# Attention in a small vision tower: ScalarE reads a pair of projection pieces in one instruction where their two PSUM banks are neighbours

## The chip, the core and the metric

The kernel runs on one core of a Trainium2 chip. The core has five engines that run side by side and meet at semaphores: TensorE (PE, matmuls, with its weight loads, PEld), VectorE (DVE), ScalarE (ACT), GpSimd (POOL) and SyncE (SP, which here only issues DMAs). TensorE writes its sums to PSUM, 8 banks of 512 fp32 numbers per partition. The metric is the time of one execution on the device in microseconds, as the median of several runs.

## The reference, cut to what matters

A batch of 64 images goes through a patch embedding, one attention layer with fake quantisation and one feed-forward layer. D = 192, 12 heads of 64, N = 197 tokens per image.

```
h = tok(x, W, b); h = concat([cls_tok, h], axis=1)              # (64, 197, 192)
a = layernorm(h)
qkv = fake_quant(a, sx1, zx1) @ fake_quant(ww1, sw1, zw1).T     # 3 x 768 columns
q, k, v = split(qkv), heads of 64
p = softmax(fake_quant(q) @ fake_quant(k).T * scale)
o = fake_quant(p, sa, za) @ fake_quant(v, sv, zv)
h = h + (fake_quant(o, sx2, zx2) @ fake_quant(ww2, sw2, zw2).T + bb2)
h = h + ffn(layernorm(h))
```

fake_quant(t, s, z) rounds t / s, adds z, clips to 0..15, and goes back. The change lies in the line qkv: in how its sums leave PSUM.

## The kernel before

Three stages follow each other: the embedding (to about 235 us), attention (to about 860 us) and the feed-forward layer over pairs of 128-row tiles. The change is in attention.

Attention is a software pipeline over images. In image step b each engine goes through six slots u = 0..5, its instructions in a fixed order written out by hand, and works on several images at once: scores and exponentials of image b, v projection of image b + 1, q and k projections of images b + 2 and b + 3 (each even step makes q of two images, each odd step k), weighted values of b - 3, output projection of b - 5. Each engine has one queue in order.

*PSUM.* Banks 0 to 3 hold scores, bank 4 the softmax sums, and banks 5, 6, 7 all the rest, in turn. This rest are 14 pieces per step, in the order of the table SLOTS:

```
SLOTS = [[("y", 0, -5), ("qk", 0, 2), ("qk", 1, 2)],
         [("qk", 2, 2), ("qk", 3, 2), ("o", 0, -3)],
         [("qk", 4, 2), ("qk", 5, 2)],
         [("v", 0, 1), ("v", 1, 1), ("o", 1, -3)],
         [("v", 2, 1), ("v", 3, 1)],
         [("o", 2, -3)]]
def bank_of(b, n): return 5 + (NP * (b + 2) + n) % 3        # NP = 14
```

An entry is kind, number of the piece, and image relative to b. A qk piece is 128 x 394 (128 output channels, two images of 197 tokens), a v piece 128 or 69 tokens x 384 channels. So each step has five pairs of projection pieces, one in each of the slots 0 to 4.

*TensorE*, slot by slot (image_slot): in slot 0 first the output projection (L1213); then the pair of the slot (function projections: two matmuls over the first 128 of 192 input channels, L1197, then two over the last 64, L1200, which run side by side in two halves of the array); then the scores of the next unit (L1247); then in even slots the softmax sums (L1260), in odd ones the weighted values (L1230). In slot 5 the weighted values come first. Before each first matmul of a piece TensorE waits until ScalarE has read the piece that last stood in the bank (before, and the semaphores in the table evac, "qk_read" and "v_read"). The last matmul of a pair adds 2 to the semaphore in the table full.

*ScalarE*, slot by slot (image_step in its block): the exponential of unit u (L625, 788 columns out of two neighbouring banks), then the pieces of the slot one by one (read_piece: qk at L587, v at L596, y at L601, o at L606), each read scaled and rounded to int16 and each adding 1 to its evac semaphore.

*VectorE* clips the int16 numbers to 4 bits and makes them bf16 (L860): the qk pieces once all six are read, the v pieces once all four are. It also scales the probabilities (L1075), with a factor that comes through DRAM (z_row).

Of the kernel before, what the change touches and what calls it, by code (L numbers as in the profile page):

```python
# [5 lines left out]
def vit_tower_kernel(nc, xt, w_tok, tok_b, cls_tok, w1t, w2t, bb2, quant, w_in_t, g_in, w_out_t, g_out,  # L6
# [11 lines left out]
    ACT = mybir.ActivationFunctionType  # L18
    AX = mybir.AxisListType

    B, N, D = out.shape
# [14 lines left out]
    with ctx:  # L36
        def sb(name, shape, dt):
            return ctx.enter_context(nc.sbuf_tensor(name, shape, dt))

        def sem(name):  # L40
            return ctx.enter_context(nc.semaphore(name))

        def wait(eng, s, value):

            if isinstance(value, int) and value <= 0:
                return
            eng.wait_ge(s, value)
# [9 lines left out]
        psum = ctx.enter_context(nc.psum_tensor("psum", [128, 8, 512], fp32))  # L57
# [12 lines left out]
        F_Q, F_K, F_V, F_EXP, F_O, F_Y = range(6)  # L70
# [42 lines left out]
        qki = sb("qki", [128, 6, 2, N], i16)  # L113
        qkb = sb("qkb", [128, 2, 12, 2, N + 1], bf16)
        vi = sb("vi", [128, 2, 2, INNER], i16)
# [47 lines left out]
        evac = {k: sem(f"{k}_read") for k in ("qk", "v", "o", "y")}  # L163
# [134 lines left out]
        def exists(b, d):  # L298

            return 0 <= b + d < B  # L300

        def bank_of(b, n):

            return 5 + (NP * (b + 2) + n) % 3
# [234 lines left out]
        def _(act):  # L539
# [33 lines left out]
            def added(image, par):  # L573

                return 32 * ((image - par) // 2) if isinstance(image, int) else 16 * (image - par)

            def read_piece(b, par, n):
                kind, k, d = PIECES[n]
                if not exists(b, d):
                    return  # L580
                im, bank = b + d, bank_of(b, n)
                ip = im % 2
                act.wait_ge(full[kind], PER[kind] * im + k + 1)
                if kind == "qk":
                    if k == 0:
                        wait(act, s_qkb, b + 2)
                    act.activation(qki[:, k, :, :], psum[:, bank, 0:2 * N]  # L587
                                   .rearrange("p (c n) -> p c n", c=2), ACT.Copy,
                                   scale=factor[(F_Q, F_K)[b % 2]])\
                       .then_inc(evac[kind], 1)  # L590
                elif kind == "v":
                    t, half = k // 2, k % 2
                    r, W = TOK[t][1], INNER // 2
                    if k == 0:
                        wait(act, s_vb, im - 1)
                    act.activation(vi[0:r, ip, t, half * W:(half + 1) * W], psum[0:r, bank, 0:W], ACT.Copy,  # L596
                                   scale=factor[F_V]).then_inc(evac[kind], 1)
                elif kind == "y":
                    if im > 1:
                        wait(act, s_added[ip], added(im, ip))  # L600
                    act.activation(att[:, ip, :, :], psum[:, bank, 0:2 * D].rearrange("p (t d) -> p t d", t=2),  # L601
                                   ACT.Copy, scale=factor[F_Y]).then_inc(evac[kind], 1)
                else:
                    if k == 0:
                        wait(act, s_ob, im - 1)
                    act.activation(oi[:, ip, 2 * k:2 * k + 2, :], psum[:, bank, 0:2 * N]  # L606
                                   .rearrange("p (c n) -> p c n", c=2), ACT.Copy,
                                   scale=factor[F_O]).then_inc(evac[kind], 1)

            act.wait_ge(s_step, CONST_STEPS)  # L610
            factor = {}
# [4 lines left out]
            def image_step(b, par, tri):  # L616
                n = 0
                for u in range(U1):
                    U = U1 * b + u
                    if exists(b, 0):  # L620
                        g, t, r = u // 2, u % 2, TOK[u % 2][1]
                        act.wait_ge(s_scores, U + 1)
                        wait(act, s_pi, 2 * b - 5 + t)

                        act.activation(ex[0:r, tri, t, 4 * g:4 * g + 4, :].rearrange("p (a h) n -> p a h n", a=2),  # L625
                                       psum[0:r, 2 * t:2 * t + 2, 0:2 * N]
                                       .rearrange("p a (h n) -> p a h n", h=2), ACT.Exp,
                                       scale=factor[F_EXP]).then_inc(s_exp, 1)
                    for _ in SLOTS[u]:
                        read_piece(b, par, n)  # L630
                        n += 1
                    if b < 0:
                        if u == 0:
                            act.wait_ge(s_xb, JOIN + b + 1)
                            act.wait_ge(s_hp, JOIN + b + 1)
                        store_tile(JOIN + b, u)
# [787 lines left out]
```

## Time and profile before

| | us |
|---|---|
| median of 3 runs | 1194.58 |
| lowest and highest | 1193.99, 1195.8 |
| the profiled execution | 1195.78 |
| its span, first to last instruction | 1194.0 |
| TensorE, VectorE, ScalarE busy in the span | 1108.2, 1056.6, 923.6 |

The profile is of one execution. Times within it count from the start of the span. The page gives busy time for the whole; the stretches give it by stage; the timeline lists instructions in order of time, neighbours of one line merged, so that the second column is the time from the first start to the last end and x the number of instructions; the waits say which engine sat idle and who released it. An engine's rows can overlap: the end of one instruction lies over the start of the next.

### The profile page before, as it was taken

The page shows a single profiled execution, that of the slowest core. Times are in us where ns is not written, and L with a number is a line of the kernel's source. Part 1 is how long each engine was busy: PE and PEld are TensorE (multiplying, and loading weights), DVE is VectorE, ACT ScalarE, POOL GpSimd, SP SyncE. Part 2 cuts the span into 40 slices and gives each one's busy share as a digit, 9 for nine tenths or more (in the row PEclk, how much of TensorE's full clock was granted, in tenths as well). Part 3 has the DMA queues.
Part 4 walks back from the last instruction along what each step waited for, and adds up shares of the span by engine and source line. Part 5 has one row for each costly group of instructions (what it writes and reads, how often), then busy time and mean ns, then how long its engine had stood idle before and what let it go on. Part 6 is the DMA issues. An engine that isn't in the chain of part 4 may idle for free.

```text
span 1194.0 us, 32030 instructions
## 1 busy us (share of the span) xinstructions
PE 1108.2 (93%) x11210; PEld 674.9 (57%) x11210; DVE 1056.6 (88%) x2028; ACT 923.6 (77%) x1832; POOL 466.1 (39%) x498
## 2 busy tenths in 40 slices
PE   7999999889999999999999999999867888888887
PEld 6999998445555555555555555555534444444444
DVE  7687666599999999999999999999887999999996
ACT  0000001889999999999999999999637999999997
POOL 5644344302211223221111232221236777766774
PEclk9999999999999999999999999999879999999999
DMA  8998998445655566556555655555532333333332
GB/s 292 313 314 249 316 306 236 137 138 150 152 150 150 131 147 156 145 150 150 145 150 147 141 150 151 149 151 143 146 98 64 105 101 101 103 99 99 99 95 71
DMA packets 157284, 187.87 MB, mean 157 GB/s; under 512 B 42864, under 2 KB 118464, under 8 KB 156928
## 3 DMA queue, kind: packets, MB, share of 16 engines
q1 hardware_dynamic: 115680, 156.92, 42.2%
q0 software_dynamic: 15936, 10.88, 9.4%
q10 hardware_dynamic: 25536, 18.31, 4.8%
q8 instruction: 83, 1.36, 0.5%
q14 instruction: 49, 0.40, 0.2%
HBM read 143.11 MB, written 36.12 MB: 150 GB/s over the span
## 4 chain that ended last, share of the span: by engine, by line
PE 73%; ACT 10%; issue 7%; DMA 3%; DVE 3%; POOL 2%; SPq 1%; ACTq 1%; DVEq 0%; POOLq 0%
PE psum L1139 14%; PE psum L1197 12%; PE psum L1260 12%; PE psum L1230 7%; PE psum L1200 7%; PE psum L1213 6%; PE psum L1247 6%; PE psum L1326 5%; ACT yi L674 3%; ACT zi L682 2%; ACT big L667 2%; PE psum L1306 1%; PE psum L1316 1%; DMA big<-xt 1%; POOL big L797 1%
## 5 line engine op out<-in xcount | busy, mean ns | idle before, releaser
L1075 DVE TENSOR_TENSOR pi<-big 128x2364 int16<-128x2364 f32 (+1 forms) x128 | 333.8, 2608 | 13.5 <-DMA big<-z_row 13.0
L769 POOL DMA_DIRECT2D h_res<-att x128 | 146.8, 1301 | 492.7 <-ACT att L601 484.0
L625 ACT ACTIVATE big<-psum 128x788 f32<-128x788 f32 (+1 forms) x384 | 330.3, 862 | 5.1 <-PE psum L1247 2.8
L587 ACT ACTIVATE qki<-psum 128x394 int16<-128x394 f32 x384 | 172.4, 508 | 25.5 <-PE psum L1200 13.8
L1139 PE MATMUL psum<-big 128*128 128x192 f32 (+1 forms) x1128 | 185.0, 327 | 2.3 <-DMA big<-xt 2.0
L1139 PEld LDWEIGHTS psum<-big 128*128 128x128 f32 (+1 forms) x1128 | 180.3, 188 | 5.5 <-DMA big<-xt 2.6
L1260 PE MATMUL psum<-big,sa_hot 128*32 128x197 f32 (+1 forms) x3072 | 168.2, 336 | 0.6 <-DVE zt L1099 0.6
L587 ACT ACT_TABLE_LOAD x1 | 1.3, 1283 | 189.5 <-PE psum L1200 189.5
L797 POOL TENSOR_TENSOR big<-big,goutb 128x512 f32<-128x512 f32 (+1 forms) x99 | 123.8, 1270 | 59.5 <-DVE big L1042 59.4
L1247 PE MATMUL psum<-qkb 64*128 64x197 bf16 (+1 forms) x1536 | 128.9, 246 | 1.3 <-DVE qkb L860 1.3
L596 ACT ACTIVATE vi<-psum 128x384 int16<-128x384 f32 (+1 forms) x256 | 115.7, 529 | 4.0 <-PE psum L1200 3.7
L1230 PE MATMUL psum<-big,vb 128*64 128x197 bf16 (+1 forms) x1536 | 104.8, 259 | 14.8 <-issue 12.9
L860 DVE TENSOR_SCALAR big<-pi,lo,hi 128x2364 bf16<-128x2364 int16 (+1 forms) x128 | 114.9, 898 | 2.4
L606 ACT ACTIVATE oi<-psum 128x394 int16<-128x394 f32 x192 | 102.7, 536 | 18.2 <-PE psum L1230 18.1
L1197 PE MATMUL psum<-xT,w1b 128*128 128x394 bf16 x384 | 105.3, 334 | 4.9 <-ACT qki L587 2.1
L1260 PEld LDWEIGHTS psum<-big,sa_hot 128*32 128x32 f32 (+1 forms) x3072 | 80.8, 109 | 42.8 <-issue 0.8
L1288 PE MATMUL psum<-winb 96*128 96x512 bf16 x428 | 103.8, 386 | 0.0
L1326 PE MATMUL psum<-winb,big 96*128 96x512 bf16 (+1 forms) x396 | 96.9, 388 | 0.0
L1247 PEld LDWEIGHTS psum<-qkb 64*128 64x128 bf16 (+1 forms) x1536 | 76.4, 104 | 31.6 <-issue 11.4
L1230 PEld LDWEIGHTS psum<-big,vb 128*64 128x64 bf16 (+1 forms) x1536 | 62.2, 111 | 56.2 <-issue 53.4
L869 DVE TENSOR_TENSOR big<-psum,tokb 128x192 f32<-128x192 f32 x98 | 34.4, 351 | 56.5 <-PE psum L1139 56.1
L1197 PE MATMUL psum<-w1b,xT 128*128 128x384 bf16 (+1 forms) x256 | 72.7, 335 | 8.5 <-ACT vi L596 1.5
(109 smaller groups left out, 1812.6 us busy)
## 6 DMA issues: line engine op xcount, KB each, us to landing
big<-z_row SPq DMA_DIRECT2D x192, 394.0 KB, 5.0
big<-xt SPq DMA_DIRECT2D x98, 384.0 KB, 4.7
tin<-h_res SPq DMA_DIRECT2D x49, 192.0 KB, 3.0
tres<-h_res SPq DMA_DIRECT2D x49, 192.0 KB, 2.5
out<-oo SPq DMA_DIRECT2D x49, 192.0 KB, 2.6
h_res<-big ACTq DMA_DIRECT2D x84, 96.0 KB, 4.5
h_res<-att POOLq DMA_DIRECT2D x64, 96.0 KB, 3.4
x_int<-big ACTq DMA_DIRECT2D x84, 64.0 KB, 4.4
```

The source lines that it names most:

```text
L587: act.activation(qki[:, k, :, :], psum[:, bank, 0:2 * N] .rearrange("p (c n) -> p c n", c=2), ACT.Copy, scale=factor[(F_Q, F_K)[b % 2]])\
L596: act.activation(vi[0:r, ip, t, half * W:(half + 1) * W], psum[0:r, bank, 0:W], ACT.Copy, scale=factor[F_V]).then_inc(evac[kind], 1)
L625: act.activation(ex[0:r, tri, t, 4 * g:4 * g + 4, :].rearrange("p (a h) n -> p a h n", a=2), psum[0:r, 2 * t:2 * t + 2, 0:2 * N] .rearrang ...
L769: pool.dma_start(h_res[bass.ds(b - 4, 1), t0:t0 + r, :].rearrange("a n d -> (a n) d"), att[0:r, par, t, :], accum_op=ALU.add).then_inc(s_a ...
L797: g.tensor_tensor(yg[0:r, oth, a, :], yy[0:r, a, 0:HID], goutb[0:r, :], ALU.mult)\
L1075: v.tensor_tensor(pi[0:r, t, :, 0:N], ex[0:r, it, t, :, :], zb[0:r, ip, :, :], ALU.mult).then_inc(s_pi, 1)
L1139: last = mm(psum[p0:p0 + r, bank_of_tile(i, s), 0:D], xring[:, s, c * 128 + p0:c * 128 + p0 + r], weight_of(cls, c), start=(c == 0), stop= ...
L1197: mm(psum[rows, bank, 0:n], left[:, 0], right[:, 0], start=True, stop=False)
L1230: last = mm(psum[i * DH:(i + 1) * DH, bank, c * N:(c + 1) * N], vb[0:r, (tri + d) % 3, t, head * DH:(head + 1) * DH], pT[0:r, im % 2, t, j ...
L1247: last = mm(psum[0:r, 2 * (w % 2) + i % 2, (i // 2) * N:(i // 2 + 1) * N], qk[po:po + DH, 6 + c, t0:t0 + r], qk[po:po + DH, c, 0:N], start ...
L1260: last = mm(psum[32 * j:32 * j + 32, 4, 0:N], sa_hot[0:r, w // 2, :], ex[0:r, it, t, 4 * (w // 2) + j, :], start=(w == 0), stop=(w == 5))
L1326: last = mm(psum[0:r, 2 * a + half, :], zT3[:, oth, a, c, 0:r], winb[:, c, half * HID:(half + 1) * HID], start=(c == 0), stop=(c == 1))
```

## The change

read_piece, on ScalarE, now looks at the banks of a pair of qk or v pieces. Where the second bank is the one above the first (5,6 or 6,7), the first call reads both pieces in one instruction (PSUM operand and int16 operand both twice as long) and adds 2 to the evac semaphore at its end, and the second call returns after its wait. Where the banks are 7 and 5, the two reads stay apart. The o and y pieces are read as before. Nothing else of the kernel is edited: TensorE's order, its waits and what they wait for are the same.

```
             act.wait_ge(full[kind], PER[kind] * im + k + 1)
+            pieces = slice(k, k + 1)
+            if kind in ("qk", "v"):
+                together = bank_of(b, n - k % 2) < bank_of(b, n - k % 2 + 1)
+                if together and k % 2:
+                    return
+                pieces = slice(k, k + 1 + together)
+            count = pieces.stop - k
             if kind == "qk":
                 if k == 0:
                     wait(act, s_qkb, b + 2)
-                act.activation(qki[:, k, :, :], psum[:, bank, 0:2 * N]
-                               .rearrange("p (c n) -> p c n", c=2), ACT.Copy,
+                act.activation(qki[:, pieces, :, :].rearrange("p k c n -> p k (c n)"),
+                               psum[:, bank:bank + count, 0:2 * N], ACT.Copy,
                                scale=factor[(F_Q, F_K)[b % 2]])\
-                   .then_inc(evac[kind], 1)
+                   .then_inc(evac[kind], count)
             elif kind == "v":
-                t, half = k // 2, k % 2
+                t = k // 2
...
-                act.activation(vi[0:r, ip, t, half * W:(half + 1) * W], psum[0:r, bank, 0:W], ACT.Copy,
-                               scale=factor[F_V]).then_inc(evac[kind], 1)
+                act.activation(vi[0:r, ip, t, k % 2 * W:(k % 2 + count) * W].rearrange("p (k w) -> p k w", k=count),
+                               psum[0:r, bank:bank + count, 0:W], ACT.Copy,
+                               scale=factor[F_V]).then_inc(evac[kind], count)
```

ScalarE before, in the middle of any image step, from the reads of slot 1 (qk 2,3) to the exponential behind the v reads of slot 4 (qki: int16 of q and k; oi: of the weighted values; vi: of v; big: the exponentials):

```order
L587 ACTIVATE qki<-psum 128x394 x2
L606 ACTIVATE oi<-psum 128x394
L625 ACTIVATE big<-psum 128x788
L587 ACTIVATE qki<-psum 128x394 x2
L625 ACTIVATE big<-psum 69x788
L596 ACTIVATE vi<-psum 128x384 x2
L606 ACTIVATE oi<-psum 128x394
L625 ACTIVATE big<-psum 128x788
L596 ACTIVATE vi<-psum 69x384 x2
```

ScalarE after, the same place in a step where the first pieces of these pairs stand in banks 6, 6, 5, 5 (P2, P3, P4, P5 in the prediction's words, layout A):

```order
L594 ACTIVATE qki<-psum 128x788
L614 ACTIVATE oi<-psum 128x394
L633 ACTIVATE big<-psum 128x788
L594 ACTIVATE qki<-psum 128x788
L633 ACTIVATE big<-psum 69x788
L603 ACTIVATE vi<-psum 128x768
L614 ACTIVATE oi<-psum 128x394
L633 ACTIVATE big<-psum 128x788
L603 ACTIVATE vi<-psum 69x768
```

All four pairs of these slots have become one instruction each. The next step, from the same place (banks 5, 5, 7, 7; layout B):

```order
L594 ACTIVATE qki<-psum 128x788
L614 ACTIVATE oi<-psum 128x394
L633 ACTIVATE big<-psum 128x788
L594 ACTIVATE qki<-psum 128x788
L633 ACTIVATE big<-psum 69x788
L603 ACTIVATE vi<-psum 128x384 x2
L614 ACTIVATE oi<-psum 128x394
L633 ACTIVATE big<-psum 128x788
L603 ACTIVATE vi<-psum 69x384 x2
```

In this step the qk reads are joined and the v reads, whose banks are 7 and 5, are not. The step after it (banks 7, 7, 6, 6; layout C):

```order
L594 ACTIVATE qki<-psum 128x394 x2
L614 ACTIVATE oi<-psum 128x394
L633 ACTIVATE big<-psum 128x788
L594 ACTIVATE qki<-psum 128x394 x2
L633 ACTIVATE big<-psum 69x788
L603 ACTIVATE vi<-psum 128x768
L614 ACTIVATE oi<-psum 128x394
L633 ACTIVATE big<-psum 128x788
L603 ACTIVATE vi<-psum 69x768
```

Here it is the other way round: the qk reads of slots 1 and 2 stand apart, the v reads are joined. The reads of qk 0,1 in slot 0 are joined in the second and third of these steps. The three kinds of step repeat to the end of attention. In all, 129 pairs of qk and 86 pairs of v are read by one instruction, of 192 and 128.

## Rows read from the trace of the kernel before

**Rows 1.** The page: busy us (share of the span) and instructions of each engine
```profile
PE 1108.2 (93%) x11210; PEld 674.9 (57%) x11210; DVE 1056.6 (88%) x2028; ACT 923.6 (77%) x1832; POOL 466.1 (39%) x498
```

**Rows 2.** Stretches: us, busy us (instructions) by engine, granted clock, DMA share, GB/s
```profile
400.00:500.00 100.00, 98.02 (x1276) 51.96 (x1274) 96.90 (x100) 97.61 (x198) 28.56 (x20) 1.00 0.62 149
```

**Rows 3.** Line 596 in 260 to 838 us: durations in ns, first and last start
```profile
L596 ACT ACTIVATE vi<-psum x232: 503/527/552, 260.9 to 837.6; 128x384 int16<-128x384 f32 x58, 69x384 int16<-69x384 f32 x58
```

**Rows 4.** Timeline of ScalarE, one image: start us, us to the last end, line, shapes
```profile
508.06 0.89 ACT L587 ACTIVATE qki<-psum 128x394 int16<-128x394 f32 x2
508.83 0.82 ACT L625 ACTIVATE big<-psum 69x788 f32<-69x788 f32 x1
509.75 0.89 ACT L587 ACTIVATE qki<-psum 128x394 int16<-128x394 f32 x2
510.52 0.51 ACT L606 ACTIVATE oi<-psum 128x394 int16<-128x394 f32 x1
510.90 0.85 ACT L625 ACTIVATE big<-psum 128x788 f32<-128x788 f32 x1
511.61 0.92 ACT L587 ACTIVATE qki<-psum 128x394 int16<-128x394 f32 x2
...
513.08 0.89 ACT L596 ACTIVATE vi<-psum 128x384 int16<-128x384 f32 x2
...
516.73 0.91 ACT L625 ACTIVATE big<-psum 128x788 f32<-128x788 f32 x1
517.51 0.50 ACT L601 ACTIVATE att<-psum 128x384 f32<-128x384 f32 x1
518.13 0.89 ACT L587 ACTIVATE qki<-psum 128x394 int16<-128x394 f32 x2
```

**Rows 5.** Timeline of TensorE's matmuls, the same image (x: instructions in the row)
```profile
508.93 0.51 PE L1197 MATMUL psum<-xT,w1b 128*128 128x394 bf16 x2
509.37 0.34 PE L1200 MATMUL psum<-xT,w1b 64*128 64x394 bf16 x2
...
509.81 0.54 PE L1230 MATMUL psum<-big,vb 128*64 128x197 bf16 x8
510.39 0.64 PE L1197 MATMUL psum<-xT,w1b 128*128 128x394 bf16 x2
...
512.22 0.50 PE L1197 MATMUL psum<-w1b,xT 128*128 128x384 bf16 x2
512.65 0.34 PE L1200 MATMUL psum<-w1b,xT 64*128 64x384 bf16 x2
...
513.08 0.54 PE L1230 MATMUL psum<-big,vb 128*64 128x197 bf16 x8
513.74 0.64 PE L1197 MATMUL psum<-w1b,xT 128*69 128x384 bf16 x2
...
515.57 0.54 PE L1230 MATMUL psum<-big,vb 128*64 128x197 bf16 x8
516.04 0.34 PE L1247 MATMUL psum<-qkb 64*128 64x197 bf16 x4
```

**Rows 6.** Timelines of both engines in narrow stretches: single instructions of those pairs
```profile
509.75 0.50 ACT L587 ACTIVATE qki<-psum 128x394 int16<-128x394 f32 x1
...
510.69 0.34 PE L1197 MATMUL psum<-xT,w1b 128*128 128x394 bf16 x1
...
514.02 0.35 PE L1197 MATMUL psum<-w1b,xT 128*69 128x384 bf16 x1
...
510.97 0.34 PE L1200 MATMUL psum<-xT,w1b 64*128 64x394 bf16 x2
```

**Rows 7.** Waits, 400 to 800 us: us, times, longest; and line 1197's loads, ns
```profile
PEld psum L1197 <- ACT vi L596: 8.3, 40, 0.2
...
L1197 PEld LDWEIGHTS psum<-xT,w1b x236: 95/97/99, 406.1 to 799.3; 128*128 128x128 bf16 x118
```

**Rows 8.** Timeline of VectorE: its one wait in that image
```profile
511.08 2.62 DVE L1075 TENSOR_TENSOR pi<-big 128x2364 int16<-128x2364 f32 x1 [0.44 <-DMA big<-z_row]
```

## The prediction

> **What bounds the kernel now.** I read the page's table of engines first: TensorE 93% busy, ScalarE 77%, VectorE 88% of the span [rows 1]. That is an average over three stages, so the next view is the stretch of 400 to 500 us, inside attention: TensorE 98.0, VectorE 96.9 and ScalarE 97.6 us busy out of 100, TensorE's granted clock at full speed [rows 2]. Three engines at 97% say nothing on who waits; the records of one image do. The reads of the v pieces come at the same place of every image: 232 of them (58 images) between 260.9 and 837.6 us, and in ScalarE's timeline one image is 518.13 - 508.06 = 10.07 us [rows 3, 4].
>
> Call the five pairs of projection pieces of an image step P1 (qk 0,1), P2 (qk 2,3), P3 (qk 4,5), P4 (v 0,1), P5 (v 2,3). Pieces go round the three banks 5, 6, 7, so a piece needs the bank of the piece three before it: P3 stands in the two banks of P2 and P5 in those of P4, each one slot earlier. There TensorE waits for ScalarE. The first read of P2 ends at 509.75 + 0.50 = 510.25 and P3's first matmul starts at 510.39, 0.14 later; the second read ends at 509.75 + 0.89 = 510.64 and P3's second matmul starts at 510.69, 0.05 later [rows 4 to 6]. P5 does the same: 513.08 + 0.53 (the median in rows 3) = 513.61 and 513.74; 513.08 + 0.89 = 513.97 and 514.02. How much of that is a stall: from the first of the eight L1230 matmuls to what follows takes 516.04 - 515.57 = 0.47 where nothing is waited for, against 0.58 before P3 and 0.66 before P5; the second matmul of a pair follows the first by 0.51 - 0.34 = 0.17 in P2's row, against 0.30 and 0.28 [rows 5, 6]. The four stalls make 0.11 + 0.13 + 0.19 + 0.11 = 0.54 us of the 10.07. The waits confirm the second place: L1197's weight loads waited for a v read 40 times in 400 us, once per image [rows 7].
>
> So the loop that sets 10.07 us has two halves. **ScalarE's half** runs from the start of P2's read (509.75) to the end of P4's second read (513.97): 4.22 us without a gap. After 0.05 us, **TensorE's half** runs from P5's second matmul (514.02) to the next P2 (508.93 + 10.07 = 519.00): 4.98 us without a stall; and 0.82 us later (509.75 - 508.93) ScalarE reads that P2. Sum: 4.22 + 0.05 + 4.98 + 0.82 = 10.07. VectorE is not in it: it still finds time to wait 0.44 us for a DMA inside the image [rows 8].
>
> **The change, part by part.** It joins two reads into one where a pair's banks are 5,6 or 6,7, and leaves them apart where they are 7,5. An image step has 14 pieces, so the pattern moves by two banks each image and repeats after three. By the order of the built kernel, layout A joins P2, P3, P4, P5; layout B P1, P2, P3; layout C P1, P4, P5: 10 of 15, and 215 of 320 pairs in the program. TensorE's order and its waits stay as they are.
>
> *What it removes.* One instruction's fixed part per joined pair. A read of 394 columns is followed by the next one 0.38 us later (510.52 to 510.90), the exponential's 788 columns take 0.71 (510.90 to 511.61), so 394 more columns cost 0.33 and the fixed part is 0.05, and a joined read ends 0.50 + 0.33 = 0.83 after its start, where two reads end after 0.89: 0.06 us earlier [rows 4]. No row shows this copy over two neighbouring banks; the exponential, which reads two banks in one instruction, lasts 0.82 to 0.91, and 0.83 is near the one that starts into an idle engine.
>
> *What it adds.* The first piece's bank is given back 0.33 us later, with the second's. TensorE, in order, can't start P3's or P5's first matmul 0.3 us ahead of the second any more: the first starts 0.14 after the joined read and the second 0.17 after that, 0.31 in all, where before the second started 0.05 after the read. A direct hand-over of a joined pair thus costs 0.31 - 0.05 - 0.06 = 0.20 us. I follow it through the image, all times as in the rows:
>
> Layouts A and B: P2's read ends at 509.75 + 0.83 = 510.58, and P3's matmuls start at 510.72 and 510.89 instead of 510.69. P3's read, behind the exponential, could begin at 511.55; P3 is full at 510.89 + 0.28 + 0.34 = 511.51, and a read starts 0.04 after its pair is full (509.37 + 0.34 = 509.71, read at 509.75): just in time. P4 follows P3 by 1.53 us as before (510.69 to 512.22): 512.42 and 512.59; P4 is full 0.26 + 0.34 later (512.65 against 512.22 + 0.17, and the length of that row), and its read starts at 513.23. Before it started at 513.08, right behind an exponential, which the joined reads now bring forward to about 512.96: ScalarE has won 0.12 us and idles 0.27 for TensorE. In B the v reads stay apart: they end at 513.73 and, 0.37 later (ten columns fewer than 0.38), at 514.10; P5's matmuls 513.87 and 514.15, **+0.13** against 514.02. In A they are joined: 513.23 + 0.82 = 514.05, matmuls 514.19 and 514.36, +0.34, less 0.01 since what follows an unstalled second matmul comes 0.27 and not 0.28 behind it: **+0.33**. Layout C: all as before up to 513.08; the joined v read ends 0.06 earlier, at 513.91; matmuls 514.05 and 514.22: +0.20, less 0.01: **+0.19**.
>
> From there on TensorE's half is the same 4.98 us, and the delay stays. Joined P1: P2's second matmul (508.93 + 0.17) needs its first bank, which comes free at 508.06 + 0.83 = 508.89 instead of 508.56, still in time. Joined P5: its banks are wanted again for y and for P1 of the next image, not before 516.04; its read, 1.83 us behind P4's, is done before that. Joined P3: P4's second matmul wants its first bank at 512.59, free at 512.41. VectorE waits for counts that now come no later than the second read did, and gains slack. Behind each joined read the skipped half's wait is still issued; its count is already reached, so I take it as nothing, and what would pay for it is the next exponential.
>
> Sum: (0.33 + 0.13 + 0.19) / 3 = 0.217 us per image. 58 images have the full pattern; of the faster first steps before 260.9 us I count two more: 60 x 0.217 = 13.0 us. Against its own execution (1195.78 us: span 1194.0 and 1.8 around it) that is 1208.8; against the median of 1194.58, **1207.6 us**.
>
> **Bounds of the sum.** If TensorE loads the weights while it waits, the 0.10 us of that load [rows 7] leaves the 0.14: A loses 0.18 of its price, B and C 0.09 each, which leaves 0.097 per image, 5.8 us, **1200.4**. If the joined read is as long as the longest exponential, 0.91 instead of 0.83 [rows 4], it costs 0.16 in A (twice in the loop), 0.08 in B and C: 0.107 more per image, 6.4 us, **1214.0**.
>
> **Rivals.** *ScalarE is the bound, and the joined reads shorten it.* For: 97.6 of 100 us busy. Then only the pairs within ScalarE's half count, P2 to P4: three in A, two in B, one in C, two per image on average, 2 x 0.06 x 60 = 7.2 us, **1187.4**, faster. Against: this needs TensorE not to wait for the first bank, and [rows 5, 6] show that wait in both places. The Trainium skill (Perfetto Trace Analysis, Optimizing Scalar/DVE Operations) states this rival's rule, that grouping into larger operations helps throughput when the engine is saturated, and right behind it the opposite one for this forecast: where ScalarE isn't saturated but causes bubbles on others, breaking instructions up lets work be done sooner. By the first the time would fall, by the second it rises; the trace has ScalarE's rows apart by 0.10 us from 509.65 to 509.75 and by 0.12 from 518.01 to 518.13, where rows of a full engine overlap by about 0.13 [rows 4], and TensorE stalled in four places, which speaks for the second.
>
> *Slack on TensorE hides it.* "Busy" there includes the ends of pipelined matmuls, and if TensorE's half had room, 0.2 us per image would vanish: **1194.6**, no change. Against: the period is 10.07 in every image, and within TensorE's half the same lines follow each other at the same steps each time (P2 and P4 to their L1200: 0.44 and 0.43 us) [rows 5].
>
> *It doesn't do what it says*, so that hardly any pair is joined: the built order shows 215, so I give it nothing.
>
> **How the numbers follow.** Forecast as worked out, 1203 to 1212: 0.64. Hidden weight load (1200.4): 0.10. Longer joined read (1214.0): 0.10. ScalarE as the bound (1187.4): 0.09. Slack (1194.6): 0.07. The range takes the first three, 1199 to 1214, 0.84. A measurement of this kernel tells about 0.2% (2.4 us) from no change: slower by more 0.84, within it 0.07, faster 0.09.
>
> **What would show it.** In the changed kernel the period should be 10.07 + 0.33, 0.13 and 0.19 in turn, 30.9 us for three. A joined read should last 0.83 to 0.87; P3's first matmul should start 0.14 behind it and the second 0.17 later; ScalarE should idle some 0.25 us before the v reads in layouts A and B. I am wrong if the three-image period is at or below 30.2, if the first matmul starts less than 0.1 behind the joined read, or if the stalls appear but the next P2 comes no later.

## The result, and the profile after

The changed kernel is slower. In the first comparison its median was 1215.12 us (1207.46 to 1217.21) against 1194.46 for the kernel before, a ratio of 1.0159 with a 95% interval of 1.0114 to 1.0205; in a second comparison (e8) it was 1211.45 against 1196.35, ratio 1.0122, 1.0098 to 1.0147. On the 1194.58 us of the prediction these ratios are 1213.6 and 1209.2 us. The profiled execution took 1214.1 us with a span of 1212.3.

The page of the changed kernel: matmuls busy a little less in a longer span, ScalarE with 1617 instructions instead of 1832 (the 215 joins):

```profile
PE 1102.4 (91%) x11210; PEld 676.5 (56%) x11210; DVE 1058.0 (87%) x2028; ACT 922.4 (76%) x1617; POOL 435.1 (36%) x498
```

ScalarE has 215 instructions less, but is busy only 1.2 us less in all ([rows 1] had 923.6), where 215 savings of 0.06 would be 12.9. Where its instructions overlap by about 0.13 us [rows 4], that end is counted once; before every gap it is counted in full, and between 300 and 800 us the busy time now falls into 161 pieces with gaps between them, before into 99. The stretch of 400 to 500 us, in the columns of [rows 2]:

```profile
400.00:500.00 100.00, 93.92 (x1238) 50.17 (x1236) 93.83 (x98) 95.29 (x162) 18.76 (x20) 1.00 0.57 143
```

TensorE is at full clock as before, and got through 1238 matmuls where it did 1276. All three engines are now less busy: 93.92, 93.83 and 95.29 us instead of 98.02, 96.90 and 97.61. No engine is fuller than before, so what grew is time in which they wait for each other.

The waits from 400 to 800 us (us in total, times, longest), to be read against [rows 7]:

```profile
PE psum L1205 <- ACT qki L594: 11.7, 26, 0.7
PE psum L1205 <- ACT vi L603: 11.2, 27, 0.4
...
ACT qki L594 <- PE psum L1208: 9.0, 51, 0.4
```

TensorE's matmuls of a projection pair (L1205, before L1197) now stand still for 0.4 us at a time, 53 times, and ScalarE's qk reads wait 51 times for TensorE, in a stretch of 39 images. Such rows of the matmuls themselves did not exist there before: the stall was short enough to show only at the weight loads. ScalarE's gaps are in part not new: before, it stood idle for 0.10 us and 0.12 us at the same qk reads [rows 4], which this view did not list; now the row of 526.68 has 0.16.

One image of layout A in the changed kernel, ScalarE and then TensorE, against [rows 4, 5]:

```profile
526.68 0.83 ACT L594 ACTIVATE qki<-psum 128x788 int16<-128x788 f32 x1 [0.16 <-PE psum L1208]
...
528.53 0.83 ACT L594 ACTIVATE qki<-psum 128x788 int16<-128x788 f32 x1
529.25 0.81 ACT L633 ACTIVATE big<-psum 69x788 f32<-69x788 f32 x1
530.19 0.81 ACT L603 ACTIVATE vi<-psum 128x768 int16<-128x768 f32 x1
```

```profile
525.79 0.51 PE L1205 MATMUL psum<-xT,w1b 128*128 128x394 bf16 x2
526.23 0.34 PE L1208 MATMUL psum<-xT,w1b 64*128 64x394 bf16 x2
...
527.65 0.50 PE L1205 MATMUL psum<-xT,w1b 128*128 128x394 bf16 x2 [0.44 <-ACT qki L594]
...
529.33 0.50 PE L1205 MATMUL psum<-w1b,xT 128*128 128x384 bf16 x2
...
531.15 0.49 PE L1205 MATMUL psum<-w1b,xT 128*69 128x384 bf16 x2 [0.41 <-ACT vi L603]
```

P2 is read in one instruction of 0.83 us (before, two in 0.89), which ends at 527.51. P3's first matmul starts at 527.65, 0.14 later, and its row of 0.50 says that the second follows 0.17 behind, where [rows 5] had a row of 0.64 with the first matmul 0.30 ahead. P4 comes at 529.33, ScalarE's exponential before it ends at 530.06 and would let the next instruction start at about 529.96, but the v read starts at 530.19: it waits for TensorE. P5 starts at 531.15, 0.15 behind the v read's end (531.00); its row of 0.49 and the 0.35 of one such matmul [rows 6] put the second 0.14 behind the first.

The period by layout is seen at P2's first row of four images on end:

```profile
505.30 0.51 PE L1205 MATMUL psum<-xT,w1b 128*128 128x394 bf16 x2
...
515.55 0.51 PE L1205 MATMUL psum<-xT,w1b 128*128 128x394 bf16 x2
...
525.79 0.51 PE L1205 MATMUL psum<-xT,w1b 128*128 128x394 bf16 x2
...
536.25 0.51 PE L1205 MATMUL psum<-xT,w1b 128*128 128x394 bf16 x2
```

These are layouts B, C and A: 10.25, 10.24, 10.46. Over the whole of attention I took the 57 regular periods, each from the start of one output projection to the next; their medians per layout are the numbers of the table below (before: 10.07 in all). In this sense the changed kernel has A 10.46, B 10.25, C 10.23, 30.95 us for three images against 30.21.

Where the 18.3 us between the two profiled spans lie: 1.15 before the first output projection, 13.9 in the 57 periods, 3.3 behind them. The last part is taken up again below.

| | A | B | C | three images | ratio of the runs (95%) |
|---|---|---|---|---|---|
| before | 10.07 | 10.07 | 10.07 | 30.21 | 1 |
| changed | 10.46 | 10.25 | 10.23 | 30.95 | 1.0159 (1.0114 to 1.0205) |
| e8, changed again | 10.47 | 10.25 | 10.23 | 30.95 | 1.0122 (1.0098 to 1.0147) |
| e1, P2 and P4 joined | 10.46 | 10.25 | 10.23 | 30.95 | 1.0148 (1.0097 to 1.0199) |
| e2, P1, P3, P5 joined | 10.14 | 10.14 | 10.07 | 30.36 | 1.0028 (1.0007 to 1.0049) |
| e3, joined, add 1 | 10.35 | 10.18 | 10.23 | 30.77 | 1.0089 (1.0051 to 1.0127) |
| e4, single, add 2 | 10.14 | 10.14 | 10.14 | 30.41 | 1.0025 (1.0006 to 1.0044) |
| e5, TensorE waits for both | 10.47 | 10.25 | 10.30 | 31.01 | 1.0147 (1.0112 to 1.0182) |
| e6, scores first | 9.90 | 9.90 | 9.90 | 29.71 | 0.9957 (0.9942 to 0.9973) |
| e9, e6 again | 9.90 | 9.90 | 9.90 | 29.71 | 0.9949 (0.9926 to 0.9972) |
| e7, scores first, joined | 10.08 | 9.97 | 10.06 | 30.10 | 1.0023 (0.9997 to 1.0048) |
| e10, scores first in slot 4 | 9.90 | 9.90 | 9.90 | 29.69 | 0.9938 (0.9918 to 0.9959) |
| e11, P1 and P5 joined, add 1 | 10.07 | 10.07 | 10.07 | 30.22 | 1.0018 (1.0000 to 1.0036) |

The times of one kernel spread by some 10 us from run to run (27 runs of the kernel before in one comparison: 1192.04 to 1202.97), while the medians of the periods repeat to 0.01 us. So the mechanism is read from the periods, and the ratio says what it comes to.

### The profile page after: what moved, and what is told of

The parts are those of the page before. It is cut to its first block, busy times and chain, and to the rows that moved or that the text cites. A ratio compares the mean times of both kernels' runs of the same rounds, so it can differ in the third digit from the quotient of the medians.

```text
span 1212.3 us, 31998 instructions
## 1 busy us (share of the span) xinstructions
PE 1102.4 (91%) x11210; PEld 676.5 (56%) x11210; DVE 1058.0 (87%) x2028; ACT 922.4 (76%) x1617; POOL 435.1 (36%) x498
## 4 chain that ended last, share of the span: by engine, by line
PE 66%; ACT 17%; issue 8%; DVE 3%; DMA 2%; POOL 2%; ACTq 1%; SPq 1%; DVEq 0%; POOLq 0%
PE psum L1147 14%; PE psum L1268 12%; PE psum L1205 11%; PE psum L1208 6%; PE psum L1221 6%; PE psum L1334 5%; PE psum L1255 5%; PE psum L1238 4%; ACT qki L594 3%; ACT yi L682 3%; ACT vi L603 3%; ACT zi L690 2%; ACT big L675 2%; PE psum L1314 1%; PE psum L1324 1%
## 5 line engine op out<-in xcount | busy, mean ns | idle before, releaser
L633 ACT ACTIVATE big<-psum 128x788 f32<-128x788 f32 (+1 forms) x384 | 317.9, 830 | 4.4 <-PE psum L1255 3.7
L777 POOL DMA_DIRECT2D h_res<-att x128 | 120.6, 1066 | 534.7 <-ACT att L609 525.3
L594 ACT ACTIVATE qki<-psum 128x394 int16<-128x394 f32 (+1 forms) x255 | 163.4, 670 | 33.1 <-PE psum L1208 28.5
L1205 PE MATMUL psum<-xT,w1b 128*128 128x394 bf16 x384 | 100.0, 334 | 22.1 <-ACT qki L594 21.0
L603 ACT ACTIVATE vi<-psum 128x768 int16<-128x768 f32 (+3 forms) x170 | 106.4, 654 | 9.2 <-PE psum L1208 4.5
L614 ACT ACTIVATE oi<-psum 128x394 int16<-128x394 f32 x192 | 95.9, 500 | 19.5 <-PE psum L1238 19.5
L1205 PE MATMUL psum<-w1b,xT 128*128 128x384 bf16 (+1 forms) x256 | 66.3, 330 | 20.1 <-ACT vi L603 19.4
```

The source lines that it names most:

```text
L594: act.activation(qki[:, pieces, :, :].rearrange("p k c n -> p k (c n)"), psum[:, bank:bank + count, 0:2 * N], ACT.Copy, scale=factor[(F_Q, ...
L603: act.activation(vi[0:r, ip, t, k % 2 * W:(k % 2 + count) * W].rearrange("p (k w) -> p k w", k=count), psum[0:r, bank:bank + count, 0:W], ...
L777: pool.dma_start(h_res[bass.ds(b - 4, 1), t0:t0 + r, :].rearrange("a n d -> (a n) d"), att[0:r, par, t, :], accum_op=ALU.add).then_inc(s_a ...
L1205: mm(psum[rows, bank, 0:n], left[:, 0], right[:, 0], start=True, stop=False)
```

## The experiments

### e1 and e2: which joins cost

```
 together = bank_of(b, n - k % 2) < bank_of(b, n - k % 2 + 1)
+    and (kind, k - k % 2) in (("qk", 2), ("v", 0))                    # e1: only P2, P4 joined
+    and (kind, k - k % 2) in (("qk", 0), ("qk", 4), ("v", 2))         # e2: only P1, P3, P5 joined
```

> The changed kernel, but only P2 and P4 are joined (where their banks are neighbours), the pairs whose banks are handed straight on to P3 and P5. P1, P3, P5 are read apart. Theory (the late hand-over of the first bank): 4 of the 10 joins in three images carry the whole loss, so three images take about 30.9 us (30.95 in the changed kernel, 30.22 before) and the run is some 14 to 18 us above before. Rival (every joined read costs, by its own length or by a slower start): 4 of 10 joins keep about 40% of the loss, three images take 30.5 us.

> The complement: only P1, P3 and P5 are joined, 6 of the 10 joins. Theory (late hand-over): none of these banks is wanted in the next slot, so three images take 30.2 us as before, within 0.05, and the run is within 0.2% of before. Rival (every joined read costs): three images take about 30.65 us, the run some 8 us above before.

P2's rows in e1, layouts B, C, A:

```profile
508.33 0.51 PE L1205 MATMUL psum<-xT,w1b 128*128 128x394 bf16 x2
...
518.58 0.51 PE L1205 MATMUL psum<-xT,w1b 128*128 128x394 bf16 x2
...
528.81 0.51 PE L1205 MATMUL psum<-xT,w1b 128*128 128x394 bf16 x2
...
539.27 0.51 PE L1205 MATMUL psum<-xT,w1b 128*128 128x394 bf16 x2
```

10.25, 10.23 and 10.46: with 4 of the 10 joins all of the loss is there, to 0.01 us. The rival, a price on every joined read, falls: it wanted 30.5 for three images here. But e2 was not what I expected: 10.14 in A and B, where P3 is joined. The reason is in its trace, ScalarE's exponential and its read of P3, and then TensorE's two matmuls of P4 in layout B:

```profile
504.30 0.85 ACT L633 ACTIVATE big<-psum 128x788 f32<-128x788 f32 x1
505.00 0.86 ACT L594 ACTIVATE qki<-psum 128x788 int16<-128x788 f32 x1
```

```profile
505.61 0.34 PE L1205 MATMUL psum<-w1b,xT 128*128 128x384 bf16 x1
...
505.92 0.34 PE L1205 MATMUL psum<-w1b,xT 128*128 128x384 bf16 x1
```

The joined read starts no later than a single one would (0.70 us behind the exponential, 0.71 in [rows 4]). It ends at 505.86, and P4's second matmul starts at 505.92, 0.31 behind the first instead of 0.17. P4's second piece stands in the bank of P3's first: a third hand-over, which I had found free at 512.41 for a matmul at 512.59 [rows 5]. That holds in the changed kernel, where the joined P2 has already delayed P4; alone, P4 wants the bank at 512.39, and the join of P3 costs 0.07 us per image in its turn. So it is the same mechanism in one place more, and the two prices don't add: the larger one covers the smaller.

### e5: the late hand-over without any join

```
 if prior := before(b, n0 + i):
-    wait(pe, evac[prior[0]], prior[1])
+    both = u in (2, 4) and i == 0 and bank_of(b, n0) < bank_of(b, n0 + 1)
+    wait(pe, evac[prior[0]], prior[1] + both)
```

> The kernel before, no read joined, one thing added: where the change would join P2 (or P4), TensorE's first matmul of P3 (or P5) waits until both pieces of that pair are read, not the first alone. The late hand-over by itself, without the 0.06 us that a join saves. Theory: P3's first matmul starts 0.14 us behind the second read's end (510.64), its second 0.17 later, 510.95 instead of 510.69. Worked through as in the prediction: layout A +0.41, B +0.17, C +0.24 on 10.07 us, three images 31.04 us (30.95 in the changed kernel), the run some 15 us above before. Rival (the joined read itself costs, not the hand-over): the period stays near 10.07.

```profile
507.84 0.51 PE L1198 MATMUL psum<-xT,w1b 128*128 128x394 bf16 x2
...
518.08 0.51 PE L1198 MATMUL psum<-xT,w1b 128*128 128x394 bf16 x2
...
528.38 0.51 PE L1198 MATMUL psum<-xT,w1b 128*128 128x394 bf16 x2
...
538.84 0.51 PE L1198 MATMUL psum<-xT,w1b 128*128 128x394 bf16 x2
```

By the medians of the periods B +0.18, C +0.23, A +0.40, where the working gave 0.17, 0.24 and 0.41. No read is joined here, ScalarE's instructions are those of the kernel before, and three images take 31.01 us, 0.80 more than before. This is the proof of the main step: a first matmul that has to wait for both reads is enough for a loss of this size. That it is nearly the changed kernel's 0.74 is in part chance, since two smaller terms of that kernel, taken apart below, almost cancel.

### e3 and e4: what adding 2 costs

The changed kernel's joined reads start later than I had worked out: in layout A P2's read starts 526.68 - 525.79 = 0.89 us after P2's first matmul, in [rows 4, 5] it was 0.82. In its trace none of the 215 reads that add 2 to their semaphore carries a wait (in the kernel before, all 640 single reads do); the wait is an instruction of its own ahead of it. e3 keeps the joins and adds 1 (the waiters count reads); e4 joins nothing and adds 2:

```
-   .then_inc(evac[kind], count)                 # changed
+   .then_inc(evac[kind], 1)                     # e3; waits: reads(kind, pieces)
-   .then_inc(evac[kind], 1)                     # before, qk and v
+   .then_inc(evac[kind], 2)                     # e4; waits: twice the count
```

> The changed kernel with the same joined reads, but a joined read adds 1 to its semaphore and the waiters count reads instead of pieces. In the changed kernel's trace a joined read adds 2, has no wait of its own, and its wait is a separate instruction: it starts 0.107 us after its pair is full where a single read starts 0.042 after. If adding 2 is the cause, the wait goes back into the read, P2's joined read starts 0.82 and not 0.89 us after P2's first matmul, and three images take 30.95 - 0.19 = 30.76 us (0.067 in A and B for P2, 0.06 in A for P4): 3.6 us less per run. If the width of the read is the cause, all stays at 0.89 and 30.95.

> The kernel before, with every read of a qk or v piece alone as before, but each adds 2 to its semaphore and all waits for these counts are doubled. The disputed cost by itself: if adding 2 splits the wait off the read, P2's first read starts 0.89 instead of 0.82 us after P2's first matmul, the period rises from 10.07 by 0.07 to 0.13 us and the run by 4 to 8 us. If adding 2 costs nothing, the period stays at 10.07.

e4, TensorE's P2 and ScalarE's first read of it:

```profile
521.53 0.51 PE L1197 MATMUL psum<-xT,w1b 128*128 128x394 bf16 x2
...
531.67 0.51 PE L1197 MATMUL psum<-xT,w1b 128*128 128x394 bf16 x2
```

```profile
522.42 0.50 ACT L587 ACTIVATE qki<-psum 128x394 int16<-128x394 f32 x1
```

0.89 instead of 0.82 from matmul to read, and a period of 10.14 instead of 10.07: 0.07 us for each image, with nothing else changed. e3 takes them back:

```profile
567.40 0.51 PE L1232 MATMUL psum<-xT,w1b 128*128 128x394 bf16 x2
...
577.58 0.51 PE L1232 MATMUL psum<-xT,w1b 128*128 128x394 bf16 x2
...
587.82 0.51 PE L1232 MATMUL psum<-xT,w1b 128*128 128x394 bf16 x2
...
598.16 0.51 PE L1232 MATMUL psum<-xT,w1b 128*128 128x394 bf16 x2
```

B 10.18, C 10.24, A 10.34; the sum by the medians is 30.77, where 30.76 was expected. So 0.18 of the 0.74 us that the change costs in three images come from the split wait. The other 0.56 are the late hand-over less what the shorter reads give back: e5, which has the hand-over alone, stands at 0.80, and 0.24 less is what the four joins of P2 and P4 should save at 0.06 each.

### e6, e7, e9, e10: filling the stall

```
+if u in (2, 4):                    # e6, e7, e9; in e10: if u == 4
+    scores(b, par, u)
+    projections(b, u)
-if u < 5:
+elif u < 5:
     projections(b, u)
     scores(b, par, u)
```

> The kernel before with one exchange in TensorE's order: in slots 2 and 4 the four score matmuls (L1247) stand ahead of the pair P3 or P5 and not behind it, so TensorE has 0.26 us of work where it stalled 0.24 and 0.30 us for ScalarE's reads. Theory (TensorE waits there for the banks): P3 and P5 start as early as before or nearly so, what stands behind them comes 0.27 us earlier, and TensorE's half shortens by that: period 9.80 to 9.90 instead of 10.07, the run 10 to 16 us faster than before. Rival (another engine bounds at 10.07, such as VectorE with its 9.63 us of work plus a DMA wait): period 10.0 to 10.07, no change.

> The kernel of e6 once more (the kernel before with the scores ahead of P3 and P5), in more rounds. Its trace has a period of 9.90 us, 9.6 us less in 57 periods; its twelve runs had a median only 5 us below before. If the period decides, the ratio is 0.992; if the rest of the program gives part of it back, 0.995 to 0.996.

> The exchange of e6 in slot 4 alone (scores ahead of P5, not ahead of P3). Theory of the two halves: slot 4 is where TensorE's half begins, so the exchange there shortens the loop by about 0.17 us, and the stall before P3 lies beside ScalarE's half and is free: period 9.90, as with both. Rival (TensorE is the bound and every stall counts): only the part of one stall goes, period 9.98.

Slot 4 in e6: the scores L1247 now lie ahead of P5, and the softmax sums L1260 follow it:

```profile
508.98 0.36 PE L1247 MATMUL psum<-qkb 64*69 64x197 bf16 x4
509.29 0.64 PE L1197 MATMUL psum<-w1b,xT 128*69 128x384 bf16 x2
509.86 0.35 PE L1200 MATMUL psum<-w1b,xT 64*69 64x384 bf16 x2
```

P5 still waits for the two v reads (its row is 0.64 long), since ScalarE's half has not changed, but behind it 0.17 us are gone: 9.90 us per image, the upper end of what was expected. The expected 0.27 was too much, because the sums follow L1200 after 510.14 - 509.86 = 0.28 us where the scores followed after 0.19 (514.50 - 514.31 in the kernel before). e10 has the same 9.90 with slot 4 alone, two of its rows of P2:

```profile
526.95 0.51 PE L1197 MATMUL psum<-xT,w1b 128*128 128x394 bf16 x2
...
536.85 0.51 PE L1197 MATMUL psum<-xT,w1b 128*128 128x394 bf16 x2
```

That confirms the two halves: the stall before P3 lies beside ScalarE's half and is free, the one before P5 is where the loop passes to TensorE. These are the fastest kernels of the case, 0.4 to 0.6% faster than before (e10: 1189.74 us against 1196.35). The 5 to 6.6 us by the medians are less than the 10 to 16 expected of e6, and less than 57 periods of 0.17 would give. In the profiles the 57 periods take 10.1 us less in e6, 7.3 in e9 and 5.6 in e10. In e10 a few of them take 10.1 to 11.95 us, and its longest wait for the softmax factor's DMA is 3.6 us (2.4 before), in this row of VectorE:

```profile
DVE pi L1075 <- DMA big<-z_row: 11.1, 11, 3.6
```

I have not tried what is behind that, nor why e6, with all 57 periods at 9.90, gains only 5.0 us by its median.

> The exchange of e6 together with the joined reads of e3 (add one). With the stalls filled, the late hand-over is partly covered: worked through, layout B gains 0.12 against e6, A loses 0.08, C loses 0.20, 0.05 us per image more than e6 on average, 3 us per run more than e6. If joined reads help once TensorE doesn't stall (ScalarE then the bound), it is 0.1 us per image faster than e6.

```profile
511.69 0.51 PE L1232 MATMUL psum<-xT,w1b 128*128 128x394 bf16 x2
...
521.75 0.51 PE L1232 MATMUL psum<-xT,w1b 128*128 128x394 bf16 x2
...
531.82 0.51 PE L1232 MATMUL psum<-xT,w1b 128*128 128x394 bf16 x2
...
541.79 0.51 PE L1232 MATMUL psum<-xT,w1b 128*128 128x394 bf16 x2
```

C 10.06, A 10.07, B 9.97: 0.13 us per image slower than e6, not 0.05. The direction held on average, but not in layout B, which was to gain 0.12 and lost 0.07; A lost 0.18 instead of 0.08, C 0.16 instead of 0.20. I had left P3's hand-over to P4, the one that e2 shows, out of that sum. It is there, in P4's rows of layouts C, A and B:

```profile
514.85 0.50 PE L1232 MATMUL psum<-w1b,xT 128*128 128x384 bf16 x2
...
525.05 0.57 PE L1232 MATMUL psum<-w1b,xT 128*128 128x384 bf16 x2
...
535.12 0.57 PE L1232 MATMUL psum<-w1b,xT 128*128 128x384 bf16 x2
```

Where P3 is joined (A and B) P4's second matmul comes 0.07 later. That is less than the 0.10 and 0.19 us by which A and B missed the sum; the rest I have not followed. Even with the stalls filled the joins give back most of what the exchange had won: 0.39 of the 0.50 us in three images, and by the ratio, 1.0023 (0.9997 to 1.0048), no gain is left.

### e11: joins that nobody waits for

```
 together = ... and (kind, k - k % 2) in (("qk", 0), ("v", 2))          # P1, P5; adds 1
```

> Only P1 and P5 are joined where their banks are neighbours, each joined read adding 1: neither's banks are wanted within the next slot, and neither lies in ScalarE's half. Theory: period 10.07 in all three layouts, within 0.01, run as before within 0.2%; that ScalarE saves 0.06 us per join brings nothing. Rival (ScalarE's work is the bound): period 10.07 - 0.08 = 9.99, the run 4 to 5 us faster.

```profile
503.19 0.51 PE L1232 MATMUL psum<-xT,w1b 128*128 128x394 bf16 x2
...
513.26 0.51 PE L1232 MATMUL psum<-xT,w1b 128*128 128x394 bf16 x2
```

10.07, to 0.01 as expected. What ScalarE saves here is won outside its half of the loop and turns into waiting. The ratio, 1.0018 (1.0000 to 1.0036), is no gain either.

### e8: the changed kernel again, and the clock

> The changed kernel once more, in more rounds and beside the others of this call, since its first four runs spread from 1207.5 to 1217.2 us. By its trace attention's 57 regular periods cost 13.9 us more than before. If that is all, the ratio to before is 1.012; if the dips of TensorE's granted clock around the end of attention also last longer in it, it is 1.015 to 1.016, as first measured.

The periods repeat (30.95), and the ratio of 1.0122 is what the 13.9 us of the periods come to by themselves (1.2%). The runs show what goes with the higher first comparison: each has a mean granted clock of TensorE, as a share of full speed, and its span goes with it. The changed kernel's ten runs go from 1215.4 us at 0.979 and 1214.4 at 0.980 to 1205.7 at 0.990 (correlation -0.96); the kernel before goes from 1199.9 at 0.978 to 1189.6 at 0.991. The first four runs had 0.983 on average, the six of e8 0.9855. Where the clock is 0.986 to 0.988 the changed kernel's four runs take 1207.3 to 1209.8 us, the 31 of the kernel before 1193.8 in the median: 15 us apart, and not the 20.7 between the first two medians.

The profiled spans of the two kernels differ by 3.3 us behind attention's regular part too. There, while attention runs out and the feed-forward layer starts, TensorE's granted clock falls to 1.2 GHz for several us at a time, in every kernel here. Stretches of 120 us from about the same point (before; changed), where the granted clock is the third number from the end:

```profile
839.00:959.00 120.00, 94.88 (x762) 52.40 (x759) 102.55 (x260) 84.06 (x162) 61.87 (x74) 0.90 0.39 99
```

```profile
854.00:974.00 120.00, 96.91 (x747) 53.61 (x744) 98.78 (x249) 80.74 (x153) 59.41 (x71) 0.84 0.36 98
```

0.84 in the changed kernel (0.86 in e8), 0.90 before, but also 0.90 in e1, whose attention is as slow, and its span is 3.7 us shorter than the changed kernel's. Behind the 57 periods, leaving out the last dip at the program's end, TensorE was at 1.2 GHz for 23.9 us before and in e1, 37.5 in the changed kernel and 34.1 in e8; that part of the span took 355.4, 351.8, 358.6 and 357.1 us. Over the 13 profiles the one goes with the other: the least time at 1.2 GHz, 17.1 us in e2 and e9, stands beside 350.9 and 352.1, and e4, which joins nothing, has 30.7 and 358.1. So long dips need no joined read, and the 3.3 us are not shown to be the change's. Nor is the clock all of it, since the kernel before and e1 differ by 3.6 us at the same 23.9.

## Why the prediction was right

**The bound and the loop.** The two halves, 4.22 and 4.98 us, carried e5's three periods and e3's sum to 0.01 us and e10's and e11's periods; they missed e2 by 0.07 in two layouts and e7 by 0.10 and 0.19. Reading only busy shares (97.6% for ScalarE) would have led to the rival of 1187.4. It falls by the changed kernel's own periods, which are longer in all three layouts, although pairs within ScalarE's half are joined in each; e11 adds that work taken off ScalarE outside its half gains nothing. The Trainium skill's first rule of that section (Perfetto Trace Analysis, Optimizing Scalar/DVE Operations) is bound to a saturated engine. By these runs ScalarE at 97.6% was not one, and its second rule, of an engine that causes bubbles on others, is the one that fits: joining cost 0.74 us in three images in e1, where TensorE waits for the pieces, and nothing in e11, where nobody does.

**The joined read.** Worked out as 0.83 us; the groups of the changed kernel from 400 to 800 us (count, busy us, mean ns, idle before) have

```profile
L594 ACT ACTIVATE qki<-psum 128x788 int16<-128x788 f32 x78 | 64.5, 827 | 9.2 <-PE psum L1208 9.0
...
L603 ACT ACTIVATE vi<-psum 128x768 int16<-128x768 f32 x26 | 21.2, 817 | 1.7
```

0.827 and 0.817 us on average. The bound of 0.91 was not needed. P3's first matmul starts 0.14 behind the read and the second 0.17 later, as stated, so the bound with the hidden weight load falls too. It had the reason for the 0.14 wrong. In the kernel before, the median weight load of such a first matmul starts only 0.113 us behind ScalarE's read and the matmul 0.03 after that, so the load's 0.10 us don't lie ahead of it. What lies ahead is again a wait that is an instruction of its own, here on TensorE; the second matmul's load carries its wait and starts 0.051 us behind its read. The changed kernel and e5 have the same 0.113 to 0.114.

**The layouts.** A +0.33, B +0.13, C +0.19 were forecast, +0.39, +0.18 and +0.16 measured: 0.65 against 0.74 in three images, and in the 57 regular periods 12.4 us (13.0 was for 60 images) against 13.9. The term that was missing is the start of the joined read: I costed the wait that is left over from the skipped half, rightly at nothing (e11), and did not ask what adding 2 does to the wait of the read itself. e4 puts it at 0.07 us per hand-over from an idle ScalarE, e3 at 0.18 in three images. Without it the measured sum is 0.56, below the 0.65 forecast: the rest of the working was 0.09 too high (by e3's periods, 10.35, 10.18 and 10.23: about 0.05 in A, 0.02 in B, 0.03 in C). 0.03 of that in A and in C is P5's second matmul, which I had 0.17 behind the first and which came 0.14 behind. That the sum came within 0.09 is therefore luck in part: a term of 0.18 was missing and terms of 0.09 were too large, on opposite sides. The mechanism does not hang on it; e5 and e1 show that by themselves.

**The joins said to be free.** P1 and P5 are (e11). P3 is only in the presence of the joined P2 (e1 without its join has the changed kernel's 30.95; e2 with it, but without P2's, loses 0.07): a step that was right for the change as it stands and would have been wrong for a part of it.

**The total.** 1207.6 was forecast with 1199 to 1214 around it; 1213.6 and 1209.2 by the two ratios, and the first median by itself, 1215.12, lies 1.1 us above the range. The upper end of the range stood on a joined read of 0.91 us, which did not come: that 1213.6 lies inside is luck, while 1209.2 lies in the forecast as worked out (1203 to 1212). The periods make 13.9 of it, the split wait included; the rest lies before and behind attention's regular part, where the prediction had three images' worth (0.65 us) and no term for the clock, and where runs of one kernel spread by 10 us.

## What to carry to other kernels

Joining two instructions of a reader saves its fixed part (0.06 us here) and gives the first buffer back as late as the second (0.33 us): before joining, look who waits for the first buffer and how soon, and where the loop passes from one engine to the other. Where two engines at 97% hand work back and forth, find the half of the loop that each of them carries; only work taken out of a half, or moved into a stall at its border as in e10, shortens it. A read that adds 2 to its semaphore lost the wait that was attached to it (0.07 us per hand-over in e4): compare the rows of the first instruction after an idle time before and after.

## What the runs showed of the hardware

On ScalarE an ACTIVATE that adds 2 to a semaphore had no wait attached in any trace here (215 in the changed kernel, 640 in e4); the wait ran as a separate instruction, and the read began 0.11 us after the end of the last matmul it waited for (526.23 + 0.34 = 526.57 to 526.68 in layout A) where with a wait of its own it began 0.04 after it. From P2's first matmul to its read it took 0.89 us in e4 and in the changed kernel, 0.82 in the kernel before and in e3. Where the piece was full before the instruction ahead had run out, no such delay shows: e2's joined read of P3, which adds 2, starts 0.70 us behind the exponential, as single reads do (0.71).

TensorE has the same difference of 0.06 us. Behind ScalarE's read, the weight load of a pair's first matmul starts 0.113 us later where a separate wait instruction stands ahead of it, and 0.051 us later where the load carries the wait (medians in the kernel before, 300 to 800 us).
